# One attention block and one expert layer on one core: the transposes of the probabilities stand in front of the weighted sums instead of behind them

## The chip, the cores and the metric

The kernel runs on 1 core of one Trainium2 chip. The metric is the device time in microseconds (us) from start to end; lower is better. Engines are named as the profile names them: PE is TensorE (matmuls and transposes), PEld its weight loads, DVE is VectorE, ACT is ScalarE, POOL is GpSimd, SP issues DMAs.

## The reference

Two gated blocks follow each other on x of 32 batches x 128 tokens x 256.

```python
# cross attention, 16 heads of 64; scores and probabilities are 128 x 128 for each batch and head
q, k, v = layernorm(x) @ Wq, ctx @ Wk, ctx @ Wv
probs = softmax(q @ k.T / 8)
x = x + tanh(g_x) * ((probs @ v) @ Wo + bo)
# mixture of 8 experts, the best 2 for each token, with a capacity for each expert
logits = layernorm(x) @ gate_w.T
x = x + tanh(g_f) * sum over 2 experts of gate * (relu(row @ fc1 + b1) @ fc2 + b2)
```

## The kernel before

The attention takes the first 60% of the span, the experts the rest. The change is in the attention alone.

**Steps.** The 32 batches are 8 groups `g` of 4 (512 tokens). For a group the 16 heads go in 8 pairs, so there are 64 steps: step `u` is pair `j = u % 8` of group `u // 8`. In a step PE makes the queries of pair u, the keys of pair u+1 and a part of the values of step u+2, then the scores of pair u, and the weighted sums of pair u-2. `misc_of(u)` adds other work of a group's end to some steps: output projection (O0, O1), transposes for the second layer norm (XA, XB), routing (LT, LX, PR), and in the last step of a group (j = 7) the transposes FA and FB of the next group's normalised x.

**Order.** Each engine runs a program written out by hand, in order; engines tell each other by semaphores. Nothing is scheduled by a tool. PE's `step(u)` before: `transpose_probs(u-2)`, `query(u)`, keys, values, misc, `scores(u)`, `weigh_values(u-2)`. As the next step begins with `transpose_probs(u-1)`, PE meets scores (u), weighted sums (u-2), transposes (u-1), query products (u+1).

**Shapes in the PE array.** Query products and transposes use all 128 rows and columns of the array (128\*128 in the trace). The scores contract over 64, two heads side by side in the rows (64\*128). The weighted sums write 64 partitions, two heads side by side in the columns (128\*64). The names in the trace are `query_bank<-xT,w_split` (L515 to L517), `score<-k_sb,q_sb` (L598), `out_bank<-pT,v_sb` (L586, weighted sums), `probT<-ident,work` or `probs_odd` (L573, transposes).

**Around them.** DVE's step u: maxima of the scores of u-1 (L1025), `probs_out(u-2)`, which copies the two transposed banks `probT` to `pT` in SBUF (L1033), scaling of the first half of the probabilities u-1 by their sums (L1040), the low part of the attention output u-3 (`aT_l`, L904), scaling of the second half (L1040). In steps with j = 6 and 7 the routing stands between these; in steps with j = 7 the low parts `xT_l` of the next group's x follow. ACT's step u: exponentials of u-1 (L820), high part of the attention output u-3 (`aT_h`, L774), queries out (`q_sb`), keys and values out. `scores(u)` waits for `q_sb` and for the exponentials of u-1. `weigh_values` reads `pT`. `transpose_probs` waits for both scalings. There is one `pT` and one `out_bank`.

**After step 63** `finish()` transposes the probabilities of pair 62, does the weighted sums of 62 and 63 and projects the last group in pieces between them.

Of the kernel before, what the change touches and what calls it, by code (L numbers as in the profile page):

```python
# [132 lines left out]
def attention(nc, ctx, block, sem, x_v, out_v, disp, ctxT, g_x, g_f, wq, wk, wv, wo, bo, gateT, fc1T, fc2, shared):  # L133
# [86 lines left out]
    def misc_done(kind, g):  # L220

        return {
            "O0": (s_o_done, 2 * g - 1), "O1": (s_o_done, 2 * g), "XA": (s_xa_done, g), "XB": (s_xb_done, g),
            "LT": (s_lt_done, g), "LX": (s_lg_done, g), "PR": (s_pr_done, g), "GC": (s_gc_done, 1),
            "FA": (s_f_split, 2 * g + 3), "FB": (s_f_split, 2 * g + 4),
        }[kind]
# [274 lines left out]
    def _(pe):  # L501
# [64 lines left out]
        def transpose_probs(w):  # L566
            for hh in range(2):
                pe.wait_ge(s_p_ready, 2 * w + hh + 1)
                pe.wait_ge((s_pt_done0, s_pt_done1)[hh], w)
                if hh == 1 and w % NP == NP - 2 and w < STEPS - 2:  # L570
                    pe.wait_ge(*misc_done("FB", w // NP))
                for b in range(GB):
                    last = nc.tensor.transpose(probT[hh][:, b * P:(b + 1) * P], probs[w % 2][:, hh * GB + b, :], ident[:, :])  # L573
                last.then_inc(s_pt_ready, 1)
# [91 lines left out]
        def step(u):  # L666

            kinds, w, i = misc_of(u), u - 2, u + V_AHEAD
            if w >= 0:
                transpose_probs(w)  # L670
            query(u)
            if u == 0:
                keys_main(0)
                keys_rest(0)
                pe.wait_ge(s_v_done, 1)
                values_main(value_bank, i)
                keys_main(1)
            else:
                if u + 1 < STEPS:
                    keys_main(u + 1)  # L680
                if i < STEPS:
                    pe.wait_ge(s_v_done, i)
                    values_main(value_bank, i)
            if kinds:
                pe.wait_ge(s_q_done, u + 1)
                misc(kinds[0], query_bank, u // NP)
            if kinds[1:] == ["FB"]:
                pe.wait_ge(s_pt_done1, w + 1)
                misc("FB", probT[1], u // NP)
            elif kinds[1:]:  # L690
                pe.wait_ge(s_at_split, w)
                misc(kinds[1], out_bank, u // NP)
            if u + 1 < STEPS:
                keys_rest(u + 1)
            if i < STEPS:
                values_rest(value_bank, i)
            scores(u)
            if w >= 0:
                if kinds[1:] and kinds[1] != "FB":
                    pe.wait_ge(*misc_done(kinds[1], u // NP))  # L700
                else:
                    pe.wait_ge(s_at_split, w)
                weigh_values(w)
# [4 lines left out]
        def finish():  # L708

            def project_pairs(pairs, batches):  # L710

                for j in pairs:
                    pe.wait_ge(s_at_split, STEPS - NP + j + 1)
                    for b in batches:
                        o, t = last_bank(b)[:, 0:D], slice(b * P, (b + 1) * P)
                        mm(o, aT_h[:, j, t], wo_h[:, j, :], start=(j == 0), stop=False)
                        mm(o, aT_h[:, j, t], wo_l[:, j, :], start=False, stop=False)
                        last = mm(o, aT_l[:, j, t], wo_h[:, j, :], start=False, stop=(j == NP - 1))
                        if j == NP - 1 and b % 2 == 1:
                            last.then_inc(s_o_ready, 1)  # L720

            def transpose_x1(half):

                pe.wait_ge(s_o_done, 2 * NG - 1 + half)
                pe.wait_ge((s_pt_done0, s_pt_done1)[half], 8 * NG)
                for k in range(DK):
                    for b in range(2):
                        last = nc.tensor.transpose(probT[half][:, (2 * k + b) * P:(2 * k + b + 1) * P],
                                                   x1[:, 2 * half + b, k * P:(k + 1) * P], ident[:, :])
                last.then_inc(s_xt_ready, 1)  # L730

            def logits_half(half):

                pe.wait_ge(s_xa_done, NG + half)
                for b in (2 * half, 2 * half + 1):
                    for k in range(DK):
                        last = mm(out_bank[:, b * E:(b + 1) * E], xn2T[:, k, b * P:(b + 1) * P], gate_sb[:, k, :],
                                  start=(k == 0), stop=(k == DK - 1))
                last.then_inc(s_lg_ready, 1)

            early, late = (0, 1), (2, 3)
            transpose_probs(STEPS - 2)
            pe.wait_ge(s_v_done, STEPS)
            project_pairs((0, 1), early)
            pe.wait_ge(s_at_split, STEPS - 2)
            weigh_values(STEPS - 2)
            project_pairs((2, 3, 4, 5), early)
            transpose_probs(STEPS - 1)
            project_pairs((6,), early)
            pe.wait_ge(s_exp, 16 * NG)  # L750
            project_pairs((0,), late)
            weigh_values(STEPS - 1)
            project_pairs((1, 2), late)
            project_pairs((7,), early)
            project_pairs((3, 4), late)
            transpose_x1(0)
            project_pairs((5, 6), late)
            logits_half(0)
            project_pairs((7,), late)
            ranks(key_bank, halves[0], NG)  # L760
            transpose_x1(1)
            logits_half(1)
            pe.wait_ge(s_pr_done, NG)
            ranks(key_bank, halves[1], NG + 1)
            wait_warm(60)
# [6 lines left out]
    def _(act):  # L772
        def high(out_, in_, scale=1.0):
            return nc.scalar.activation(out_, in_, ACT.Copy, scale=scale)  # L774
# [60 lines left out]
        def step(u):  # L835

            g, kinds = u // NP, misc_of(u)
            if u > 0:
                exponentials(u - 1, 0)
            if u > 2:  # L840
                attention_high(u - 3)
            if u > 0:
                exponentials(u - 1, 1)
            act.wait_ge(s_q_ready, u + 1)
            high(q_sb[:, :], query_bank[:, :], SCALE).then_inc(s_q_done, 1)
            if "XA" in kinds:
                act.wait_ge(s_xt_ready, 2 * g - 1)
                high(xn2T[:, 0, :], query_bank[:, :]).then_inc(s_xa_done, 1)
            if "LT" in kinds:
                act.wait_ge(s_lt_ready, g)  # L850
                high(logitsT[:, :], query_bank[:, 0:P]).then_inc(s_lt_done, 1)
            if "PR" in kinds:
                act.wait_ge(s_gdiff, g)
                act.wait_ge(s_disp_done, g)
                nc.scalar.activation(packed[:, :, D + 1], route.gdiff[:, :], ACT.Exp).then_inc(s_gexp, 1)
            if g > 0 and u % NP == NP - 1:
                normalise_x1((2, 3), packed[:, 2:4], s_shift2, g).then_inc(s_xn2_ready, 1)
            if "FA" in kinds:
                for k in range(DK):
                    act.wait_ge(s_f_ready, 2 * g + 3 + k)  # L860
                    high(xT_h[:, k, :], (query_bank, probT[1])[k][:, :]).then_inc(s_f_hi, 1)
            if u == 0:
                keys_out(0)
            if u + 1 < STEPS:
                keys_out(u + 1)
            if u + V_AHEAD < STEPS:
                values_out(u + V_AHEAD)
            if "PR" in kinds:
                normalise_x1((0, 1), packed[:, 0:2], s_shift2, g)
            if u == 1:  # L870
                gates()
# [26 lines left out]
    def _(dve):  # L898
# [3 lines left out]
        def low(out_, full, high_):  # L902

            return V.tensor_tensor(out_, full, high_.bitcast(f32), ALU.subtract)  # L904
# [124 lines left out]
        def probs_out(w):  # L1029

            for hh, pt_done in enumerate((s_pt_done0, s_pt_done1)):
                dve.wait_ge(s_pt_ready, 2 * w + 1 + hh)
                V.tensor_copy(pT[:, hh, :], probT[hh][:, :]).then_inc(pt_done, 1)  # L1033

        def scale_probs(w, hh):
# [20 lines left out]
        def step(u):  # L1056
# [34 lines left out]
            if has_next and j == NP - 1:  # L1091
                for k in range(DK):
                    dve.wait_ge(s_f_hi, 2 * g + 3 + k)
                    low(xT_l[:, k, :], (query_bank, probT[1])[k][:, :], xT_h[:, k, :]).then_inc(s_f_split, 1)
            if has_prev and j == 2:
                residual_start(g)
                residual(g, query_bank, 0)
# [389 lines left out]
```

## Time and profile before

| what | value |
|---|---|
| median of 3 runs | 967.03 us (964.99 to 967.63) |
| profiled execution | 967.71 us, its span 966.0 us |
| PE busy | 942.8 us, 98% of the span |
| DVE busy | 654.8 us, 68% |
| ACT busy | 520.3 us, 54% |
| mean granted clock of TensorE | 0.989 of full speed |

A row of the timeline gives start, length, engine, line and operation, the tiles written and read, and how many instructions are merged; brackets at its end give the idle time before it and what ended it. A matmul's length reaches to its modelled end, and the next one starts before that, so of PE the starts are read. A share of busy time near 100% therefore says that nothing was waited for, not that no time is lost between matmuls.

### The profile page before, as it was taken

What the parts mean: (1) busy time and instruction counts of PE and PEld (TensorE: products, weight loads), DVE (VectorE), ACT (ScalarE), POOL (GpSimd) and SP (SyncE); (2) the same over time, 40 slices, a digit from 0 to 9 for tenths busy, and PEclk for the clock granted to TensorE, in tenths of its full rate; (3) what the DMA queues carried; (4) which work ended last, traced back from release to release, by engine and by line L of the source; (5) the groups of instructions that cost most, each with busy time, mean ns of one, the idle gap of its engine ahead of it and who ended that gap; (6) DMA issues with size and microseconds to landing.
All of it is one profiled execution on the core that took longest, in us unless ns stands there. A gap on an engine that the chain in (4) does not pass through costs nothing.

```text
span 966.0 us, 19023 instructions
## 1 busy us (share of the span) xinstructions
PE 942.8 (98%) x7221; PEld 826.1 (86%) x7221; DVE 654.8 (68%) x1533; ACT 520.3 (54%) x1611; POOL 282.8 (29%) x302
## 2 busy tenths in 40 slices
PE   8998999999999999999999889999999999999996
PEld 6787889889889888888898768999999999999995
DVE  3884795795885886867847756665757575757572
ACT  5774584783783774756847524343434343535351
POOL 5912024133142223243122340223232323222222
PEclk9999999999999999999999979999999999999998
DMA  9095320120021021012001114525252626252521
GB/s 267 12 295 134 110 66 30 39 67 35 34 73 61 2 77 57 25 45 64 13 34 45 43 59 164 137 44 137 45 141 41 147 42 147 46 146 56 128 45 22
DMA packets 63099, 76.65 MB, mean 79 GB/s; under 512 B 6030, under 2 KB 55093, under 8 KB 63008
## 3 DMA queue, kind: packets, MB, share of 16 engines
q1 hardware_dynamic: 50720, 59.18, 20.5%
q0 software_dynamic: 12288, 16.25, 9.2%
q8 instruction: 58, 0.95, 0.4%
q14 instruction: 33, 0.27, 0.1%
HBM read 46.52 MB, written 29.49 MB: 79 GB/s over the span
## 4 chain that ended last, share of the span: by engine, by line
PE 93%; DMA 2%; DVE 2%; ACT 1%; issue 0%; POOL 0%; DVEq 0%; POOLq 0%
PE probT L573 6%; PE down L1346 6%; PE down L1344 6%; PE down L1345 6%; PE out_bank L586 6%; PE up L1330 6%; PE up L1331 6%; PE up L1332 6%; PE score L598 6%; PE query_bank L515 3%; PE query_bank L517 3%; PE query_bank L516 3%; PE key_bank L540 3%; DMA rows<-x_dram 2%; PE probT L125 2%; PE rT L1314 1%
## 5 line engine op out<-in xcount | busy, mean ns | idle before, releaser
L1380 ACT ACTIVATE hid<-up,b 128x512 f32<-128x512 f32 x128 | 88.3, 690 | 203.7 <-PE up L1332 131.1
L1286 POOL DMA_INDIRECT out_dram<-eo,index x64 | 103.1, 1610 | 281.1 <-DVE eo L1448 249.7
L1025 DVE TENSOR_REDUCE negmax<-score 128x4 f32<-128x512 f32 x128 | 82.2, 684 | 42.3 <-PE score L598 42.2
L820 ACT ACTIVATE probs_odd<-score,negmax 128x128 f32<-128x128 f32 x256 | 91.1, 383 | 24.7 <-DVE negmax L1025 24.7
L774 ACT ACTIVATE k_sb<-key_bank 128x512 f32<-128x512 f32 x64 | 38.7, 604 | 120.8 <-PE key_bank L540 119.6
L419 POOL DMA_INDIRECT disp<-packed,slots x56 | 57.0, 1018 | 158.8 <-DMA disp<-packed,slots 108.1
L820 ACT ACTIVATE work<-score,negmax 128x128 f32<-128x128 f32 x256 | 91.2, 383 | 16.7 <-DVE negmax L1025 16.0
L1440 DVE TENSOR_TENSOR hid_l<-hid,hid_h 128x512 fp32r<-128x512 f32 x128 | 88.6, 692 | 4.4
L1033 DVE COPY pT<-probT 128x512 f32<-128x512 f32 x128 | 82.2, 683 | 13.4 <-PE probT L573 13.4
L1448 DVE SCALAR_TENSOR_TENSOR eo<-down,gate,shares_b 128x256 f32<-128x256 f32 x64 | 29.5, 481 | 85.4 <-PE down L1346 85.4
L1438 DVE CAST hid_h<-hid 128x512 fp32r<-128x512 f32 x128 | 55.5, 434 | 38.1 <-ACT hid L1380 36.5
L598 PEld LDWEIGHTS score<-k_sb,q_sb 64*128 64x128 f32 x1024 | 66.7, 187 | 7.1 <-ACT q_sb L774 4.7
L1344 PE MATMUL down<-w_h,hid_h 128*128 128x256 f32 x256 | 72.6, 284 | 0.0
L1344 PE MATMUL down<-w_split,hid_h 128*128 128x256 f32 x256 | 72.6, 284 | 0.0
L1346 PE MATMUL down<-w_h,hid_l 128*128 128x256 f32 x256 | 72.0, 281 | 0.0
L1345 PE MATMUL down<-w_l,hid_h 128*128 128x256 f32 x256 | 71.9, 281 | 0.0
L1345 PE MATMUL down<-w_split,hid_h 128*128 128x256 f32 x256 | 71.9, 281 | 0.0
L1346 PE MATMUL down<-w_split,hid_l 128*128 128x256 f32 x256 | 71.9, 281 | 0.0
L598 PE MATMUL score<-k_sb,q_sb 64*128 64x128 f32 x1024 | 68.5, 273 | 2.4 <-ACT q_sb L774 2.3
L586 PE MATMUL out_bank<-pT,v_sb 128*64 128x128 f32 x1008 | 69.0, 279 | 0.2 <-DVE aT_l L904 0.2
L586 PEld LDWEIGHTS out_bank<-pT,v_sb 128*64 128x64 f32 x1008 | 53.7, 136 | 7.9 <-DVE aT_l L904 0.4
L820 ACT ACTIVATION_READ_ACCUMULATOR work<-score,negmax 128x1 f32 x256 | 57.0, 223 | 0.0
(294 smaller groups left out, 2769.6 us busy)
## 6 DMA issues: line engine op xcount, KB each, us to landing
rows<-disp SPq DMA_DIRECT2D x18, 516.0 KB, 4.6
w_raw<-fc1T_dram SPq DMA_DIRECT2D x9, 1024.0 KB, 7.7
w_raw<-fc_dram SPq DMA_DIRECT2D x9, 1024.0 KB, 10.4
disp<-fixed SPq DMA_DIRECT2D x1, 8256.0 KB, 34.1
rows<-x_dram SPq DMA_DIRECT2D x16, 512.0 KB, 5.3
out_dram<-rows SPq DMA_DIRECT2D x8, 512.0 KB
c_raw<-ctxT_dram SPq DMA_DIRECT2D x8, 256.0 KB, 4.4
c_raw<-ctxT_dram SPq DMA_DIRECT2D x16, 128.0 KB, 5.0
```

Of the source, the lines that this page charges most:

```text
L573: last = nc.tensor.transpose(probT[hh][:, b * P:(b + 1) * P], probs[w % 2][:, hh * GB + b, :], ident[:, :])
L586: last = mm(bank[hh * DH:(hh + 1) * DH, b * P:(b + 1) * P], v_sb[:, j // 4, b, cols], pT[:, hh, b * P:(b + 1) * P], start=True, stop=True)
L598: last = mm(score[hh][:, t], q_sb[r, t], k_sb[u % 2][r, t], start=True, stop=True)
L820: last = nc.scalar.activation(probs[w % 2][:, c, :], score[hh][:, b * P:(b + 1) * P], ACT.Exp, bias=negmax[:, w % 2, c:c + 1], accum_out=s ...
L1025: V.tensor_reduce(negmax[:, w % 2, hh * GB:(hh + 1) * GB], score[hh][:, :].rearrange("p (i k) -> p i k", i=GB), axis=AX, op=ALU.max, negat ...
L1033: V.tensor_copy(pT[:, hh, :], probT[hh][:, :]).then_inc(pt_done, 1)
L1286: pool.indirect_dma_start(out=out_rows[:, :], out_offset=bass.IndirectOffsetOnAxis(ap=index[half][:, i:i + 1], axis=0), in_=eo[half][:, i, ...
L1344: mm(o, hid_h[:, k, t], w2_h[par][:, k, :], start=(k == 0), stop=False)
L1345: mm(o, hid_h[:, k, t], w2_l[par][:, k, :], start=False, stop=False)
L1346: last = mm(o, hid_l[:, k, t], w2_h[par][:, k, :], start=False, stop=(k == HK - 1))
L1380: nc.scalar.activation(hid[m % 2][:, :], up[m % 2][:, :], ACT.Relu, bias=b1[par][:, m:m + 1]).then_inc(s_hid, 1)
L1440: V.tensor_tensor(hid_l[:, m, :], hid[m % 2][:, :], hid_h[:, m, :].bitcast(f32), ALU.subtract).then_inc(s_hid_split, 1)
```

## The change

`transpose_probs` is called one step sooner, between `scores` and `weigh_values`. PE now meets scores (u), transposes (u-1), weighted sums (u-2), query products (u+1). Because the weighted sums of u-2 now come behind the transposes of u-1, DVE's copy of the new transposes waits until those sums have read `pT` (`s_av_ready`). FB no longer borrows `probT[1]` but `out_bank`: it waits for the attention output to be out of that bank, and the weighted sums of that step wait until FB has been read.

```diff
@@ transpose_probs
-                if hh == 1 and w % NP == NP - 2 and w < STEPS - 2:
-                    pe.wait_ge(*misc_done("FB", w // NP))
@@ step(u) of PE
-            if w >= 0:
-                transpose_probs(w)
             query(u)
...
-            if kinds[1:] == ["FB"]:
-                pe.wait_ge(s_pt_done1, w + 1)
-                misc("FB", probT[1], u // NP)
-            elif kinds[1:]:
+            if kinds[1:]:
                 pe.wait_ge(s_at_split, w)
                 misc(kinds[1], out_bank, u // NP)
...
             scores(u)
+            if w >= -1:
+                transpose_probs(w + 1)
             if w >= 0:
-                if kinds[1:] and kinds[1] != "FB":
+                if kinds[1:]:
                     pe.wait_ge(*misc_done(kinds[1], u // NP))
                 else:
                     pe.wait_ge(s_at_split, w)
@@ finish() of PE
-            transpose_probs(STEPS - 2)
@@ ACT, FA and FB
-                    high(xT_h[:, k, :], (query_bank, probT[1])[k][:, :]).then_inc(s_f_hi, 1)
+                    high(xT_h[:, k, :], (query_bank, out_bank)[k][:, :]).then_inc(s_f_hi, 1)
@@ probs_out(w) of DVE
                 dve.wait_ge(s_pt_ready, 2 * w + 1 + hh)
+                if w > 0:
+                    dve.wait_ge(s_av_ready, w)
                 V.tensor_copy(pT[:, hh, :], probT[hh][:, :]).then_inc(pt_done, 1)
@@ DVE, FA and FB
-                    low(xT_l[:, k, :], (query_bank, probT[1])[k][:, :], xT_h[:, k, :]).then_inc(s_f_split, 1)
+                    low(xT_l[:, k, :], (query_bank, out_bank)[k][:, :], xT_h[:, k, :]).then_inc(s_f_split, 1)
```

On PE, at the end of a plain step (the fifth, u = 4) and the start of the next, there stood before:

```order
107 L540 MATMUL key_bank<-c_d,wk_e 128x512
108 L559 MATMUL value_bank<-wv_e,c_t 128x512
109 L598 MATMUL score<-k_sb,q_sb 128x128 x8
110 L586 MATMUL out_bank<-pT,v_sb 64x128 x8
111 L573 MATMUL probT<-ident,probs_odd 128x128 x8
112 L515 MATMUL query_bank<-xT_h,w_split 128x512
```

Now there stands:

```order
107 L540 MATMUL key_bank<-c_d,wk_e 128x512
108 L559 MATMUL value_bank<-wv_e,c_t 128x512
109 L596 MATMUL score<-k_sb,q_sb 128x128 x8
110 L571 MATMUL probT<-ident,probs_odd 128x128 x8
111 L584 MATMUL out_bank<-pT,v_sb 64x128 x8
112 L515 MATMUL query_bank<-xT_h,w_split 128x512
```

The transposes and the weighted sums have changed places, and the query products now follow the weighted sums.

On PE, at the end of the second group (u = 15), the change gives this order, in which FB (the second row of L563) is in `out_bank` and the weighted sums (L584) wait for its readers:

```order
422 L563 MATMUL query_bank<-ident,rows 128x128 x4
423 L563 MATMUL out_bank<-ident,rows 128x128 x4
424 L540 MATMUL key_bank<-c_d,wk_e 128x512
425 L559 MATMUL value_bank<-wv_e,c_t 128x512
426 L596 MATMUL score<-k_sb,q_sb 128x128 x8
427 L571 MATMUL probT<-ident,work 128x128 x8
428 L584 MATMUL out_bank<-pT,v_sb 64x128 x8
```

Before, the second row of L563 wrote `probT`, and the last two rows stood the other way round.

On DVE the order is the same; only the copy of `probT` has one more wait:

```order
36 L1019 TENSOR_REDUCE negmax<-score 128x4 [waits a_s_ready] x2
37 L1029 COPY pT<-probT 128x512 [waits a_av_ready,a_pt_ready] x2
38 L1034 RECIPROCAL rsum<-sums 128x4 [waits a_exp]
39 L1036 TENSOR_TENSOR probs_odd<-probs_odd,rsum 128x512 [waits a_dve_self]
```

## Rows read from the trace of the kernel before

**Rows 1.** The page, part 1: busy time and share of each engine.

```profile
PE 942.8 (98%) x7221; PEld 826.1 (86%) x7221; DVE 654.8 (68%) x1533; ACT 520.3 (54%) x1611; POOL 282.8 (29%) x302
```

**Rows 2.** Timeline of PE, end of step 2 and start of step 3.

```profile
32.87 1.06 PE L598 MATMUL score<-k_sb,q_sb 64*128 64x128 f32 x16
33.85 1.09 PE L586 MATMUL out_bank<-pT,v_sb 128*64 128x128 f32 x16
34.88 1.09 PE L573 MATMUL probT<-ident,probs_odd 128*128 128x128 f32 x8
35.73 0.47 PE L515 MATMUL query_bank<-xT_h,w_split 128*128 128x512 f32 x1
36.04 0.39 PE L516 MATMUL query_bank<-xT_l,w_split 128*128 128x512 f32 x1
```

**Rows 3.** Timeline of PE, end of steps 0 and 1 (no weighted sums).

```profile
21.94 1.05 PE L598 MATMUL score<-k_sb,q_sb 64*128 64x128 f32 x16
22.92 0.50 PE L515 MATMUL query_bank<-xT_h,w_split 128*128 128x512 f32 x1
23.26 0.40 PE L516 MATMUL query_bank<-xT_l,w_split 128*128 128x512 f32 x1
...
27.20 1.16 PE L598 MATMUL score<-k_sb,q_sb 64*128 64x128 f32 x16 [0.38 <-ACT q_sb L774]
28.29 1.10 PE L573 MATMUL probT<-ident,work 128*128 128x128 f32 x8
```

**Rows 4.** Timeline of PE in finish(): projection, weighted sums, projection.

```profile
550.74 0.28 PE L718 MATMUL score<-w_split,aT_l 128*128 128x256 f32 x1
550.95 1.09 PE L586 MATMUL key_bank<-pT,v_sb 128*64 128x128 f32 x16
551.97 0.39 PE L716 MATMUL score<-w_split,aT_h 128*128 128x256 f32 x1
```

**Rows 5.** Timeline of DVE, steps 3 and 4.

```profile
35.57 1.29 DVE L1033 COPY pT<-probT 128x512 f32<-128x512 f32 x2 [0.33 <-PE probT L573]
...
39.56 0.69 DVE L1040 TENSOR_TENSOR work<-work,rsum 128x512 f32<-128x512 f32 x1
```

**Rows 6.** Timeline of ACT, step 3.

```profile
36.06 0.61 ACT L774 ACTIVATE aT_h<-out_bank 128x512 fp32r<-128x512 f32 x1
```

**Rows 7.** Timeline of all engines, end of step 9.

```profile
82.13 0.66 PE L573 MATMUL probT<-ident,work 128*128 128x128 f32 x4
83.67 0.75 DVE L908 BATCH_NORM_STATS2 stats<-rows 128x6 f32<-128x256 f32 x2 [4.72 <-DMA rows<-x_dram]
...
85.28 0.98 PE L573 MATMUL probT<-ident,work 128*128 128x128 f32 x4 [2.50 <-DVE work L1040]
```

**Rows 8.** Window behind that wait (last: granted clock, DMA share, GB/s).

```profile
85.40:88.90 3.50, 3.50 (x11) 2.92 (x12) 3.47 (x7) 3.04 (x16) 1.80 (x2) 0.51 0.08 27
```

**Rows 9.** Timeline of PE and DVE, steps 15 and 16.

```profile
139.22 1.09 PE L586 MATMUL out_bank<-pT,v_sb 128*64 128x128 f32 x16
...
139.75 0.68 DVE L904 TENSOR_TENSOR xT_l<-probT,xT_h 128x512 fp32r<-128x512 f32 x1
...
144.47 0.50 PE L540 MATMUL key_bank<-c_d,wk_e 64*128 64x512 f32 x1
...
145.00 1.16 PE L598 MATMUL score<-k_sb,q_sb 64*128 64x128 f32 x16
```

**Rows 10.** Timeline of PE and DVE, step 52.

```profile
453.10 1.05 PE L598 MATMUL score<-k_sb,q_sb 64*128 64x128 f32 x16
...
454.16 0.69 DVE L1040 TENSOR_TENSOR probs_odd<-probs_odd,rsum 128x512 f32<-128x512 f32 x1
```

**Rows 11.** Timeline of PE and DVE, step 63 and finish().

```profile
539.98 1.16 PE L598 MATMUL score<-k_sb,q_sb 64*128 64x128 f32 x16 [1.96 <-ACT q_sb L774]
...
543.99 0.68 DVE L904 TENSOR_TENSOR aT_l<-out_bank,aT_h 128x512 fp32r<-128x512 f32 x1
...
544.73 1.09 PE L586 MATMUL out_bank<-pT,v_sb 128*64 128x128 f32 x16 [0.15 <-DVE aT_l L904]
```

## Prediction

> **What bounds the kernel now.** I read the page first. PE is busy 98% of the span and DVE 68% [rows 1]. Almost nothing is waited for on PE, so time can only be won or lost in what PE's own instructions cost, and in the few places where it does wait. The change adds and removes no matmul, no copy and no DMA. It is a question of order.
>
> So the second view is the timeline of PE around the place of the change, read by the starts. In a plain step the scores start at 32.87, the weighted sums at 33.85, the transposes at 34.88, the query products at 35.73, and the second query product at 36.04 [rows 2]: 0.98, 1.03, 0.85 and 0.31 us, 3.17 together. These distances are not all work. The 16 scores last 1.06 with a modelled length of 0.27 for one (my reading of a single matmul; the sum needs only starts), so their last one starts about 0.79 behind the first, at 33.66. The first weighted sum starts 0.19 later, though within the group one starts every 0.05. The last weighted sum starts about 0.82 behind the first, at 34.67, and the first transpose again 0.21 later. But the last of the 8 transposes starts at about 35.70, and the first query product 0.03 later. The array's shape changes at the first two places (64\*128 to 128\*64, 128\*64 to 128\*128) and not at the third. That is what I build on: a change of shape costs about 0.15 to 0.2 us of PE, hidden by nothing, in a stage that PE bounds.
>
> This is also what the Trainium skill says in "TensorEngine Tiling (Array Packing)", Key Properties: changing the tiling mode, and not only the tile, drains the engine. It speaks against this change and gives no figure; the trace agrees, with some 0.20 us between last and first start at a change of shape and 0.03 us where none is.
>
> **The change part by part: the swap on PE.** Before, a step has the shapes 128\*128 (queries, keys, values), 64\*128 (scores), 128\*64 (sums), 128\*128 (transposes, then queries): three changes. Now it is 128\*128, 64\*128 (scores), 128\*128 (transposes), 128\*64 (sums), 128\*128: four. The trace has no step in the new order, but it has nearly each seam.
>
> - Scores to a 128\*128 shape: 0.98 in step 0, from 21.94 to 22.92, where query products follow at once [rows 3]. The transposes of step 1 also follow scores, 1.09 behind a group that had a wait of its own inside [rows 3]. I take 0.98, as to the weighted sums.
> - Transposes to weighted sums: 0.82 from first to last transpose, and then the seam. A 128\*128 projection before weighted sums shows 0.21, from 550.74 to 550.95 [rows 4]. Together 1.03.
> - Weighted sums to a 128\*128 shape: 1.03 to transposes [rows 2], 1.02 to the projection, from 550.95 to 551.97 [rows 4]. I take 1.03.
> - First to second query product behind a change of shape: 0.34, from 22.92 to 23.26 [rows 3], instead of 0.31.
>
> The sum is 0.98 + 1.03 + 1.03 + 0.34 = 3.38 us against 3.17: **0.21 us more** for each swap. Bounds: nothing, if no seam costs by shape, and 0.30, if the two unseen seams cost half as much again as those seen.
>
> **Where it counts.** There are 62 swaps, one behind the scores of each step from 2 to 63. Not all of them lie on the path.
>
> - Steps 2 to 8 (7 swaps, 1.5 us): at the end of step 9 PE waits 2.50 us in the middle of the transposes, for a scaling that DVE does only behind statistics of x that a DMA brings at 83.67 [rows 7]. DVE had been idle for 4.72 us for that load. The end of the wait is set by the load, so these 1.5 us vanish in it: 0. If the load came later because its issue waits for FB (5 swaps ahead of it), it would be 1.0; I take 0, as it lands 16 us after PE's work for it, behind other transfers.
> - Step 9: the weighted sums stood ahead of this wait and now stand behind it. That costs their 1.03, the seam before them (0.21 instead of 0.03), and 0.03 behind: **+1.2 us**.
> - Steps 10 to 60: 51 swaps by 0.21, **+10.7 us**.
> - Steps 61 and 62: the scores of step 63 wait 1.96 us for ACT's `q_sb` [rows 11], a chain that comes from DVE and ACT. Both swaps are covered: 0. Without that cover 0.4.
>
> **The new waits.** (a) DVE's copy of the transposes now waits for the weighted sums, which end last. Before, it started at 35.57, with the first four transposes done [rows 5]. Now the sums start at 32.87 + 0.98 + 1.03 = 34.88 and end 1.09 later, so the copy starts at 36.0 to 36.05: 0.45 later. Behind it on DVE are the scalings of the next probabilities. The second one starts at 39.56 and lasts 0.69 [rows 5], so it ends at 40.25, or 40.7 if nothing absorbs the delay. The new transposes come 0.98 behind scores that start one step after 32.87, at 39.45 to 39.7; their second half needs this scaling 0.44 after that, near 41.0. Cover 0.3 or more: cost 0. (b) ACT's high part of the attention output starts at 36.06 [rows 6], when its exponentials are done; the sums now end at about 36.0. Cost 0. (c) In step 52 DVE is late: the second scaling ends at 454.85 [rows 10]. The new transposes' second half could start at 453.10 + 0.98 + 0.44 + 0.21 = 454.7. With the 0.45 of (a) it waits until 455.3: **+0.6**. Before, the weighted sums covered this. (d) FB in `out_bank`: weighted sums of the last step of a group wait for `xT_l`, which ends at 140.43 [rows 9], or 140.75 with DVE some 0.3 later. They could start at 139.22 + 1.03 + 0.21 = 140.45. That is 0.3 to 0.35 of new wait in the five groups with routing on both sides. But the scores of the next step then waited already: they started 0.53 behind the last part of the keys (144.47 to 145.00) [rows 9], where 0.33 is usual, and 0.1 more inside. A PE that comes later doesn't wait there. Net 0 to -0.1 each: **-0.5** for all. (e) In `finish()` the weighted sums of 62 wait for the low part of 61, made at 543.99 behind the copy of the transposes, and start at 544.73 [rows 11]. That copy is 0.45 later as in (a), and so are they: **+0.5**.
>
> **Sum:** 10.7 + 1.2 + 0.6 - 0.5 + 0.5 = 12.5 us on the profiled execution, which took 967.7 us (span 966.0). That execution is 0.7 us above the median of 967.0, so I forecast 967.0 + 12.5, about **979.5 us**.
>
> One thing can take back a part: behind the 2.50 us wait the granted clock was 0.51 for 3.5 us, near the lower of its two levels (1.2 of 2.4 GHz) [rows 8], which cost about 1.4 us. The wait changes too: the sums no longer stand ahead of it, and PE comes to it 1.5 us later, so it is 2.50 + 1.03 - 1.5 = 2.0 us. With less idle time the clock may not fall: -1.4. A wait of 1.96 us [rows 11] is as long, and I leave it open.
>
> **The rivals.**
>
> - *DVE becomes the bound.* The 0.45 us of (a) goes round: copy, scaling, transposes, and the second half of the transposes waits in each step. For it: DVE's chain from score to scaling takes most of a step. Against it: the cover of 0.3 worked out above, which grows by 0.21 with each slower step of PE. Price: 0.25 more in 51 steps, 12.8 us, 992 us. It decides from the point where DVE's second scaling comes over 0.3 later than I think.
> - *The seam isn't due to the shape*, but belongs to any group behind several waits, and the order changes nothing on PE. Then only the stalls remain: 1.2 - 0.2 + 0.6 - 0.5 + 0.5 = 1.6 us, 968.6 us. Against it: transposes and query products also have waits in front, and there it is 0.03.
> - *Faster: a drain is paid only between the two split shapes.* If transposes to sums and sums to query products came at the group's own pace (0.05 instead of 0.2 at both seams), a step would be 0.98 + 0.87 + 0.88 + 0.31 = 3.04, 0.13 less than before. 51 times that is -6.6, with 1.6 of stalls: 962 us. It decides from the point where both seams together are under 0.22. Against it are sums to projection, 1.02 [rows 4], and scores to query products, 0.98 [rows 3], which show the full seam. The one seam never seen is transposes to sums.
>
> **How the numbers follow.** My forecast (four changes of shape instead of three) has 0.80, DVE as the bound 0.08, no change on PE 0.07, faster 0.05. A change of 0.3% (2.9 us) is about what a measurement of this kernel can tell from none. Slower by more: 0.80 + 0.08 = 0.88. Within: 0.07. Faster: 0.05. The range of the likeliest case: from 0.15 for a swap (7.7 instead of 10.7) and a clock that doesn't fall, 967.0 + 12.5 - 3.0 - 1.4 = 975, to 0.26 for a swap, the load 1.0 later and 1 us of waits more, 984. I give 973.5 to 985, a little wider for the waits that I took as covered.
>
> **What would show it.** In the trace after: scores to transposes 0.98, transposes to sums 1.03, sums to query products 1.03 by the starts, and a plain step 0.21 us longer. The copy of `probT` starts 0.45 later behind the scores. PE's waits stay few: the one at the end of step 9 near 2.0 us, one in step 52, short ones at L584 in the last step of a group. If transposes follow scores with a wait for L1036 in most steps, the first rival holds. If a plain step is as long as before, the second. What would make the prediction wrong is above all a seam from transposes to sums that costs much more or much less than the 0.21 of a projection.

## The result

The changed kernel takes 977.29 us in the median of 6 runs (975.27 to 978.68). The kernel before, run beside it, took 966.01 us (6 runs, 964.46 to 967.63). The ratio is 1.0116, with a 95% interval of 1.0100 to 1.0131: 9.7 to 12.7 us slower. The forecast was 979.5 us from a base of 967.0, which is 12.5 us slower, or a ratio of 1.013. The profiled execution spans 977.0 us, 11.0 more than before.

PE's time in the page grew by the same 11 us, and PE is still busy 98% [rows 1]:

```profile
PE 953.9 (98%) x7221; PEld 828.5 (85%) x7221; DVE 653.6 (67%) x1533; ACT 521.3 (53%) x1611; POOL 280.4 (29%) x302
```

The timeline of PE at the end of step 2 of the changed kernel answers to [rows 2]:

```profile
32.65 1.06 PE L596 MATMUL score<-k_sb,q_sb 64*128 64x128 f32 x16
33.64 1.09 PE L571 MATMUL probT<-ident,probs_odd 128*128 128x128 f32 x8
34.66 1.09 PE L584 MATMUL out_bank<-pT,v_sb 128*64 128x128 f32 x16
35.68 0.50 PE L515 MATMUL query_bank<-xT_h,w_split 128*128 128x512 f32 x1
36.02 0.40 PE L516 MATMUL query_bank<-xT_l,w_split 128*128 128x512 f32 x1
```

Read by the starts: 0.99, 1.02, 1.02 and 0.34 us, 3.37 together, where the forecast had 3.38 and before it was 3.17. No bracket stands at any of these rows: nothing is waited for, and the time is lost all the same. From the scores of one plain step to those of the next it is 0.18 to 0.20 us more than before, throughout the attention (step 27 to 28: 248.65 to 255.96, 7.31; before 244.25 to 251.38, 7.13).

These are all of PE's waits over 0.3 us in the changed kernel (in total, times, longest):

```profile
PE key_bank L125 <- POOLq L340: 3.7, 1, 3.7
PE probT L571 <- DVE work L1036: 2.8, 2, 2.6
PE key_bank L618 <- DVE mask_half L958: 2.5, 2, 1.7
PE score L596 <- ACT q_sb L768: 1.8, 2, 1.5
PE probT L723 <- DVE rows L1127: 0.8, 1, 0.8
PE out_bank L732 <- ACT work L768: 0.7, 1, 0.7
PE probT L571 <- DVE probs_odd L1036: 0.5, 1, 0.5
PE out_bank L584 <- DVE aT_l L898: 0.5, 1, 0.5
```

The wait of 2.6 is the one at the end of step 9 (2.50 before, [rows 7]; the forecast had 2.0), the one of 0.5 for `probs_odd` is that of step 52, the one of 0.5 for `aT_l` that of `finish()`. The timeline around the wait of step 9, PE and DVE of the changed kernel:

```profile
82.41 0.66 PE L571 MATMUL probT<-ident,work 128*128 128x128 f32 x4
84.06 0.75 DVE L902 BATCH_NORM_STATS2 stats<-rows 128x6 f32<-128x256 f32 x2 [3.49 <-DMA rows<-x_dram]
...
85.67 0.66 PE L571 MATMUL probT<-ident,work 128*128 128x128 f32 x4 [2.61 <-DVE work L1036]
...
86.25 1.97 PE L584 MATMUL out_bank<-pT,v_sb 128*64 128x128 f32 x16
```

The weighted sums now come behind the wait. They also last 1.97 instead of 1.09, since the granted clock has fallen: a window from 86 to 88 us reads 0.56.

DVE's copy starts later behind the scores by 0.53 us, where 0.45 was expected. It started 2.70 us behind them (32.87 to 35.57, [rows 5]) and now 3.23 (32.65 to 35.88):

```profile
35.88 1.29 DVE L1029 COPY pT<-probT 128x512 f32<-128x512 f32 x2 [0.85 <-PE out_bank L584]
```

### The profile page after: what moved, and what is told of

Its sections match the earlier page's. It is cut to its first block, busy times and chain, and to the rows that moved or that the text cites. A ratio compares the mean times of both kernels' runs of the same rounds, so it can differ in the third digit from the quotient of the medians.

```text
span 977.0 us, 19149 instructions
## 1 busy us (share of the span) xinstructions
PE 953.9 (98%) x7221; PEld 828.5 (85%) x7221; DVE 653.6 (67%) x1533; ACT 521.3 (53%) x1611; POOL 280.4 (29%) x302
## 4 chain that ended last, share of the span: by engine, by line
PE 94%; DVE 3%; DMA 2%; issue 1%; ACT 0%; POOL 0%; DVEq 0%; POOLq 0%
PE out_bank L584 6%; PE probT L571 6%; PE down L1342 6%; PE down L1340 6%; PE down L1341 6%; PE up L1326 6%; PE up L1327 6%; PE up L1328 6%; PE score L596 5%; PE query_bank L515 4%; PE query_bank L516 3%; PE query_bank L517 3%; PE key_bank L540 3%; DMA rows<-x_dram 2%; PE probT L125 2%; PE rT L1310 1%
## 5 line engine op out<-in xcount | busy, mean ns | idle before, releaser
L1019 DVE TENSOR_REDUCE negmax<-score 128x4 f32<-128x512 f32 x128 | 82.2, 683 | 34.1 <-PE score L596 34.1
L584 PE MATMUL out_bank<-pT,v_sb 128*64 128x128 f32 x1008 | 69.8, 281 | 0.6 <-DVE aT_l L898 0.5
L584 PEld LDWEIGHTS out_bank<-pT,v_sb 128*64 128x64 f32 x1008 | 54.4, 138 | 11.4 <-issue 9.5
L515 PE MATMUL query_bank<-xT_h,w_split 128*128 128x512 f32 x128 | 57.4, 449 | 0.0
```

What stands on the lines that cost most here:

```text
L515: mm(query_bank[:, :], wq_h[:, k, c], xT_h[:, k, :], start=(k == 0), stop=False)
L584: last = mm(bank[hh * DH:(hh + 1) * DH, b * P:(b + 1) * P], v_sb[:, j // 4, b, cols], pT[:, hh, b * P:(b + 1) * P], start=True, stop=True)
L1019: V.tensor_reduce(negmax[:, w % 2, hh * GB:(hh + 1) * GB], score[hh][:, :].rearrange("p (i k) -> p i k", i=GB), axis=AX, op=ALU.max, negat ...
```

## The experiments

Each was run beside the kernel before. For the mixed orders, `swapped(u)` says in which steps the transposes stand ahead of the weighted sums.

**Where the swaps count.** Three kernels with the new order in some steps, DVE's added wait, and FB as before:

```diff
+        def swapped(u):
+            return 2 <= u <= 8          # s2_8; in s9: u == 9; in s10_60: 10 <= u <= 60 and u % NP != NP - 1
-            if w >= 0:
+            if w >= 0 and not swapped(u - 1):
                 transpose_probs(w)
             query(u)
...
             scores(u)
+            if swapped(u):
+                transpose_probs(w + 1)
             if w >= 0:
```

*Steps 2 to 8.* 

> The new order in steps 2 to 8 alone (7 swaps), FB as before. All theories agree on +0.19 us a swap up to the scores of step 9, +1.3 us there. Theory A (the wait at the end of step 9 is ended by a load that lands at its own time): the wait is shorter by 1.3 us, the scores of step 10 come 0.0 to 0.2 us later than before, the whole is the same within 0.3%. Theory B (the load lands later with its issue, which waits for FB behind 5 swaps): the scores of step 10 come 0.9 us later. Theory C (nothing absorbs them): 1.3 us later.

Measured: 966.81 us (10 runs) against 966.52 (25 runs), ratio 0.9998 (0.9983 to 1.0013), so -1.6 to +1.3 us. The swaps cost nothing that can be told. C's 1.3 us lies at the very end of the interval; B's 0.9 is not excluded by the times. The profile doesn't show the absorption: in that execution the load was there at 82.65 us, sooner than before, PE came later, and it didn't wait at all, so the scores of step 10 started at 100.61 in place of 102.32. The wait that was to absorb the swaps is itself of changing length. Against B, that the load lands later when it is issued later, speak the traces of SP: its issue starts at 66.74 us in the kernel before, 66.07 with step 9 alone, 68.92 here and 69.06 in the second profile of the changed kernel (below), and DVE's statistics that wait for it start at 83.67, 82.65, 82.65 and 82.43. An issue 3 us later is not followed by a later landing.

*Step 9.* 

> The new order in step 9 alone, FB as before. Theory A: the weighted sums no longer stand ahead of the wait of 2.5 us but behind it; the wait reads 3.5 us and the scores of step 10 come 1.2 us later than before (1.03 for the sums, 0.2 for the seam). If the clock's lower stretch behind the wait grows or moves, up to 0.6 us more. A theory in which only the number of seams counts: 0.2 us later.

Measured: 968.38 us (10 runs), ratio 1.0015 (0.9999 to 1.0031), 1.4 us by the ratio, with an interval of -0.1 to +3.0 (the medians are 1.9 apart). The timeline of PE shows the mechanism: the first four transposes, the wait, and the sums behind it.

```profile
80.44 0.66 PE L573 MATMUL probT<-ident,work 128*128 128x128 f32 x4
84.26 0.66 PE L573 MATMUL probT<-ident,work 128*128 128x128 f32 x4 [3.17 <-DVE work L1047]
84.85 1.23 PE L586 MATMUL out_bank<-pT,v_sb 128*64 128x128 f32 x16
```

The wait is 3.17 us where 3.5 was expected. The load landed sooner than before, as the timeline of DVE shows:

```profile
82.65 0.75 DVE L913 BATCH_NORM_STATS2 stats<-rows 128x6 f32<-128x256 f32 x2 [4.37 <-DMA rows<-x_dram]
```

So the size has to be read from the landing. In all three profiles, before, changed and this one, the transposes go on 1.61 us behind the start of these statistics. The scores of step 10 follow the statistics by 18.65 us before (83.67 to 102.32), by 19.83 here (82.65 to 102.48) and by 19.83 in the changed kernel (84.06 to 103.89): 1.18 us more, twice, against the 1.2 of the forecast and the 0.2 of a theory in which only the seams count. The granted clock fell in all three. The scatter of the old order is not small beside that: the kernel with four more waits (below) also has the old order here and a late load, and shows 18.22 (84.15 to 102.37).

*Steps 10 to 60 without the last of each group.* 

> The new order in steps 10 to 60 without those with j = 7: 45 swaps, FB as before. Theory A (one more change of the array's shape in each, 0.19 us): 45 x 0.19 = 8.6 us, 0.5 us for a wait in step 52, and about 0.3 us less at each of five group ends where waits of before are absorbed: +7.5 to +8.5 us. Theory D (the cost comes from the copies of probT that start 0.45 us later, as a chain through DVE): the cost would sit in waits for DVE that add up to most of 8 us; A expects under 2 us of them.

Measured: 975.04 us (4 runs) against 966.52, ratio 1.0080 (1.0053 to 1.0107), so 5 to 10 us with 7.7 by the ratio. From the scores of step 10 to those of step 63 the profile shows 445.97 us against 437.66, +8.3. The waits of PE from 110 to 530 us are a single row, while the 8 us are there: theory D, which puts them into waits for DVE, is out.

```profile
PE probT L573 <- DVE probs_odd L1047: 0.5, 1, 0.5
```

**All but the swap.** The changed kernel with `transpose_probs(w + 1)` put back behind `weigh_values(w)`.

```diff
             scores(u)
-            if w >= -1:
-                transpose_probs(w + 1)
             if w >= 0:
...
                 weigh_values(w)
+            if w >= -1:
+                transpose_probs(w + 1)
```

> All of the change but the swap: FB in out_bank, DVE's added wait, transposes behind the weighted sums. Theory A: shapes and their number as before, so plain steps last as long as before; but the weighted sums of the last step of a group wait for xT_l with no transposes ahead of them, 1.2 us in five groups and 0.3 to 0.4 in two, of which 0.3 us each is given back in the next step: +4 to +5 us. A theory in which the move of FB is free: 0. It tells what part of the 11 us isn't the swap's.

Measured: 971.77 us (10 runs), ratio 1.0049 (1.0036 to 1.0062), 3.5 to 6.0 us. Plain steps last as before to 0.01 us. The step with the group's end is 1.07 us longer. Its row in the timeline of PE:

```profile
138.85 1.09 PE L584 MATMUL out_bank<-pT,v_sb 128*64 128x128 f32 x16 [1.19 <-DVE xT_l L898]
```

The row of PE's waits over the whole, in seven places (five of about 1.2 us, two short ones):

```profile
PE out_bank L584 <- DVE xT_l L898: 6.5, 7, 1.2
```

**The swap alone.** The other half: all 62 swaps, FB in `probT[1]` as before, and one `transpose_probs(STEPS - 2)` less in `finish()`.

```diff
+            return 2 <= u < STEPS
...
-            transpose_probs(STEPS - 2)
             pe.wait_ge(s_v_done, STEPS)
```

> All 62 swaps, but FB stays in probT[1], so that the second half of the transposes waits for xT_l in the last step of a group. Against before. Theory A: the 11 us of the whole change, and 0.9 to 1.1 us more in five group ends, because the transposes (0.44 us of them) and not the whole group now stand ahead of that wait: +14 to +16 us. If FB's move costs in the changed kernel what it costs alone (4 to 5 us), then this one is at +6.

Measured: 979.31 us (4 runs) against 965.18 (21 runs), ratio 1.0144 (1.0129 to 1.0160), +14 us. The waits between 110 and 530 us are now for `xT_l`, 0.6 us in five steps:

```profile
PE probT L573 <- DVE xT_l L908: 2.8, 5, 0.6
PE probT L573 <- DVE probs_odd L1046: 0.3, 1, 0.3
```

In each of these five the step is 0.64 to 0.68 us longer than in the changed kernel, less than the 0.9 to 1.1 expected. So FB's move costs 4.7 us by itself (1.0049 of 966.5) and is worth 3 us inside the change (1.0144 against 1.0116; from the scores of step 10 to those of step 63 the profiles read 450.08 and 446.71, 3.4 apart). The two edits belong together: with the transposes in front, the wait for `xT_l` is covered, and in the changed kernel only 0.1 us of it is left (the weighted sums of step 15 start 1.12 us behind the transposes instead of 1.02).

**What the seam costs, and why.** Two kernels set the shape of the array against the number of waits. In the first the changed kernel takes transposes and sums in turns:

```diff
+                transpose_probs(w + 1, (0,))
...
-                weigh_values(w)
+                weigh_values(w, (0, 1))
+                transpose_probs(w + 1, (1,))
+                weigh_values(w, (2, 3))
```

> From the changed kernel: transposes and weighted sums in turns (4 transposes, half of the sums, 4 transposes, the other half), so two more changes of the array's shape in each of 62 steps, no wait added that isn't long satisfied, and the same work. Theory A (0.19 us for each further change of shape): a plain step is 0.38 us longer than in the changed kernel, over some 53 steps that aren't covered +20 us on it, +31 us on before. Theory E (the gap belongs to a group behind several waits of its own): the added half of the sums repeats waits that are long satisfied, so at most 0.19 us a step, +10 us on the changed kernel or none.

Measured: 992.01 us (4 runs), ratio 1.0262 (1.0238 to 1.0287) to the kernel before, 25.5 us above it and 15 above the changed kernel beside it (976.87, one run). That is between the 10 and the 20 of the two theories, so both sizes were missed. The timeline of PE says why:

```profile
48.22 0.66 PE L571 MATMUL probT<-ident,probs_odd 128*128 128x128 f32 x4
48.81 0.66 PE L584 MATMUL out_bank<-pT,v_sb 128*64 128x128 f32 x8
49.40 0.65 PE L571 MATMUL probT<-ident,probs_odd 128*128 128x128 f32 x4
49.98 0.66 PE L584 MATMUL out_bank<-pT,v_sb 128*64 128x128 f32 x8
50.57 0.50 PE L515 MATMUL query_bank<-xT_h,w_split 128*128 128x512 f32 x1
```

From the first transposes to the query product it is 2.35 us, where the changed kernel has 2.04 (33.64 to 35.68): 0.31 for two further changes of shape, 0.15 each. That is the gap of 0.20 less the pace of 0.05 that would stand there anyway. My 0.19 was that of the swap, which makes the second query product 0.03 later as well.

There is a row in which these seams can be counted. PEld, the weight loads, stands idle for 0.17 us ahead of the first load at each seam behind transposes or weighted sums, and its list of waits puts that down to "issue" (in total, times, longest). Before:

```profile
PEld probT L573 <- issue: 10.6, 62, 0.2
```

The changed kernel:

```profile
PEld query_bank L515 <- issue: 10.8, 62, 0.3
PEld out_bank L584 <- issue: 9.5, 57, 0.2
```

The kernel with turns:

```profile
PEld out_bank L584 <- issue: 19.9, 118, 0.2
...
PEld query_bank L515 <- issue: 10.7, 62, 0.2
PEld probT L571 <- issue: 10.4, 61, 0.2
```

62 places before, 119 in the changed kernel, 241 with turns. It is a count and not the price, and the seam behind the scores isn't in it.

But the kernel with turns repeats the waits of the sums too, so the second one takes them alone, where no shape changes:

```diff
             if w >= 0:
                 transpose_probs(w)
+            if w >= 1:
+                pe.wait_ge(s_at_split, w - 1)
+                pe.wait_ge(s_v_done, u - 1)
+                pe.wait_ge(s_pt_done0, w)
+                pe.wait_ge(s_pt_done1, w)
             query(u)
```

> The kernel before, with four satisfied waits of the weighted sums repeated between the transposes and the query products, where no change of shape is. Theory A: last transpose to first query product stays 0.03 us, the whole is the same within 0.3%. Theory E (several waits ahead of a group make the gap): about 0.15 us more in each of 61 steps, +9 us.

Measured: 967.15 us (10 runs) against 966.51 (19 runs), ratio 1.0004 (0.9988 to 1.0020). The timeline of PE in step 2:

```profile
33.90 1.06 PE L598 MATMUL score<-k_sb,q_sb 64*128 64x128 f32 x16
34.88 1.09 PE L586 MATMUL out_bank<-pT,v_sb 128*64 128x128 f32 x16
35.91 1.09 PE L573 MATMUL probT<-ident,probs_odd 128*128 128x128 f32 x8
36.76 0.47 PE L515 MATMUL query_bank<-xT_h,w_split 128*128 128x512 f32 x1
37.07 0.39 PE L516 MATMUL query_bank<-xT_l,w_split 128*128 128x512 f32 x1
```

0.98, 1.03, 0.85, 0.31: as before. The added waits are in the program as it ran (its trace has 122 instructions more, two for each of 61 steps). Four more satisfied waits cost nothing that can be measured, and theory E is out.

**Is the wait at the end of step 9 on the path?** The kernel before with one scaling moved on DVE:

```diff
+            if u == NP + 1:
+                scale_probs(u - 1, 1)
             if has_next and j == (1 if has_prev else 2):
                 dve.wait_ge(s_x_in, 16 * g + 32)
...
-            if u > 0:
+            if u > 0 and u != NP + 1:
                 scale_probs(u - 1, 1)
```

> The kernel before, in which DVE's step 9 does the second scaling ahead of the statistics of x that wait for the load. Nothing else is moved. The transposes no longer wait 2.5 us for it and the clock needn't fall behind them (about 1.4 us): -3 to -4 us if the load's lateness isn't handed on to the scores of step 10, which have 12 us of projection ahead of them; 0 if it is. It tests whether that wait is on the path at all, as the absorption of the first swaps says.

Measured: 965.23 us (10 runs) against 966.51, ratio 0.9985 (0.9972 to 0.9998), 0.2 to 2.7 us faster and less than the 3 to 4 expected. The wait of step 9 is gone, but a part comes back as a wait of the projection for `q_sb` (PE's waits):

```profile
PE query_bank L611 <- ACT q_sb L774: 1.6, 1, 1.6
```

In this profile the rest was lost at another place. The timeline of PE, step 63:

```profile
538.16 1.37 PE L598 MATMUL score<-k_sb,q_sb 64*128 64x128 f32 x16 [1.97 <-ACT q_sb L774]
539.46 1.97 PE L586 MATMUL out_bank<-pT,v_sb 128*64 128x128 f32 x16
```

Behind the wait ahead of the scores of step 63 the weighted sums last 1.97 us where the kernel before had 1.09. The window of 5 us from those scores (granted clock, DMA share and GB/s last) reads, in this kernel:

```profile
538.16:543.16 5.00, 5.00 (x44) 4.44 (x45) 3.15 (x10) 2.60 (x10) 2.55 (x3) 0.66 0.14 49
```

and in the kernel before:

```profile
539.98:544.98 5.00, 4.84 (x56) 4.36 (x58) 4.57 (x13) 3.69 (x16) 2.56 (x3) 1.00 0.14 49
```

The order of the instructions is the same there. The changed kernel was profiled once more in this place: 

> The changed kernel once more, beside the others on this chip: about +11 us, for a second reading of the wait at the end of step 9 (2.6 us in its first profile).

Measured: 976.87 us (one run), 10.4 above the kernel before beside it. The load came early, PE waited 0.2 us in step 9 instead of 2.6, and its clock didn't fall. From the scores of step 10 to those of step 63 it is 446.67 us, in the first profile 446.71. From there to the end it is 427.6 us, where the first profile had 426.4. ACT's last high part of the attention output starts 15.10 us behind the scores of step 63 instead of 13.00, although the weighted sums that it reads end at about 13.4, and PE waits for what DVE makes of it:

```profile
PE query_bank L711 <- DVE aT_l L898: 1.5, 1, 1.5
```

The granted clock is 1.00 there in both. Why ACT starts later in some executions stays open; the same wait, 1.0 to 1.6 us, stands in the profiles of steps 2 to 8, steps 10 to 60, all but the swap, the swap alone and scaling first.

**A clock that falls in some executions.** The window behind the scores of step 63 read 0.66 in five of the seven profiles with the old order there (steps 2 to 8, steps 10 to 60, all but the swap, waits, scaling first) and 1.00 in two (before, step 9). With the new order it read 1.00 in all four, behind a wait of 1.2 to 1.5 us instead of 2.0. From those scores to the next weighted sums but one (the first in `finish()`) it is 4.75 us in the two profiles at 1.00 and 6.2 to 6.4 in the five at 0.66, so the fall costs 1.4 to 1.6 us. From those scores to the end it is 426.0 us in the first two and 427.4 to 428.1 in the five; but that stretch also holds the late start of ACT told above, which made it 427.6 and 428.1 in two profiles whose clock did not fall (the changed kernel's second, the swap alone). To try whether work in the wait prevents the fall:

```diff
+            if u == STEPS - 1:
+                pe.wait_ge(s_v_done, STEPS)
+                keep_warm(nc, value_bank, wk_h[:, 0:P], wk_h[:, 0:TOK], 7)
             scores(u)
```

> The kernel before with 7 matmuls without use, 1.6 us, into the free value bank, in the wait of 2.0 us ahead of the scores of step 63. Theory F (behind this wait the granted clock falls in 5 of 7 profiles in the old order, which costs 1.7 us there): about 1 us faster in the median, 0.1%, and the granted clock of the next 5 us is 1.00. If the fall comes all the same: 0, or 0.1 us slower.

Measured: 964.23 us (11 runs) against 965.18 (21 runs), ratio 0.9991 (0.9982 to 1.0000). 

> The same, and the second scaling of step 9 ahead of the statistics that wait for x. Theory F and the reading that the wait of step 9 is on the path: 2 to 3 us faster than before, 0.2 to 0.3%, the fastest of all. If gains ahead of step 10 are lost again later: as warm alone.

Measured: 963.50 us (11 runs), ratio 0.9980 (0.9971 to 0.9989), 1.1 to 2.8 us faster than before and the lowest median of all. The windows behind the scores of step 63 in the two:

```profile
536.89:541.89 5.00, 4.87 (x56) 4.38 (x58) 4.57 (x13) 3.69 (x16) 2.56 (x3) 1.00 0.13 45
```

```profile
536.72:541.72 5.00, 4.87 (x56) 4.38 (x58) 4.58 (x13) 3.69 (x16) 2.56 (x3) 1.00 0.13 45
```

Both read 1.00, and both times agree with a fall prevented. But two of seven profiles read 1.00 without any such work, so two more don't prove it, and the gain of the first kernel has an interval that reaches to nothing.

## Why the prediction was right

The likeliest case came, and its cause is shown: one more change of the array's shape in each step, in a stage that PE bounds. Two further changes of shape cost 0.31 us together, waits added without a shape cost nothing that can be measured, and a swap in the plain steps costs its 0.19 us with no wait for DVE. The forecast of 12.5 us was 1.2 above the 11.3 between the medians. The 9 us of steps 10 to 60 stand in both profiles of the changed kernel; what comes ahead of them and behind them changes from one execution to the next, and that it adds up to little is in part luck.

By the terms of the sum, against the first profile of the changed kernel:

- *A swap, 0.21.* Measured 0.19. The three seams were as taken from the neighbours; the never seen one, transposes to sums, is 1.02 against 1.03. One thing was told wrongly: the keys and values do not stay at 128\*128, their last parts are 64\*128 like the scores [rows 9], so that change of shape lies ahead of them. It is there in both kernels and changes nothing in the sum.
- *Steps 10 to 60, 10.7 + 0.6 - 0.5 = 10.8.* Measured 433.56 us from the scores of step 10 to those of step 61 (103.89 to 537.45) against 424.52: +9.0 (433.51 in the second profile). In it are 51 swaps by 0.19, 9.7; step 52 with 0.5 instead of 0.6 (its step is 0.68 longer, less the swap); and, as what is left over, the group ends with about -1.2 instead of -0.5. There I had mis-sized two things: the weighted sums wait 0.1 us for `xT_l` and not 0.3 to 0.35, and small waits for `q_sb` ahead of FA vanish too (0.4 us of the weight loads in each of six places before, none after).
- *Step 9, +1.2.* In this profile the scores of step 10 come 1.6 us later than before, 0.4 of it because the load landed later (84.06 against 83.67); counted from the landing it is 1.18, as in the kernel with the new order in step 9 alone. So mechanism and size are right where the load is late. In the second profile of the changed kernel it landed at 82.43, PE waited 0.2 us, and this term wasn't paid. The wait forecast as 2.0 us was 2.6 and 0.2.
- *Steps 2 to 8, nothing.* Timed as 0 (-1.6 to +1.3), which fits. From the scores of step 2 to those of step 9 it is 1.5 us more, as priced; they can vanish only in an execution in which PE then waits for the load.
- *Steps 61 and 62, nothing.* Measured 0.01 us each.
- *finish(), +0.5.* The wait for `aT_l` is 0.47 us, and 0.15 before [rows 11]; from the scores of step 63 to the end it is 0.4 us more (426.4 and 426.0). In the second profile it is 1.6 more (427.6), for the late start of ACT.
- *The clock, left open.* In step 9 it fell in the first profile and not in the second: there it scatters from one execution to the next. Behind the scores of step 63 it fell in none of the four profiles with the new order and in five of seven with the old; up to about 1 us in the median (five of seven times 1.5) could come of that in favour of the change, which isn't shown and wasn't in the sum.

Of the rivals, DVE as the bound didn't come: in the second profile as in the first, PE's waits between 110 and 530 us are 0.5 to 0.6 us in one place. Its 0.45 us of delay was 0.53, and is covered but for some 0.2 us in single steps (step 3, and those with j = 6) and the 0.5 of step 52. That the seam isn't due to the shape is refuted by the kernel with four more waits, and that a drain is paid only between the two split shapes is refuted by the starts in the changed kernel (1.02 and 1.02).

## What to carry to other kernels

Where PE is busy without a gap, look at the starts of its matmuls and not at its busy share: at each change of the array's shape (64\*128, 128\*64, 128\*128) time is lost that no wait of PE shows, and it is paid as often as the loop runs. The weight loads' list of waits counts a part of such places, here those behind transposes and weighted sums. Order the groups so that equal shapes stand side by side, before thinking of which result is wanted sooner. And when a group is moved past another one, look for the waits that the other covered: each of the two edits here was dearer alone than with its partner.

## What the runs showed of the hardware that I had not expected

A change of shape between groups of 128-column matmuls costs 0.15 us of PE over the pace of the group (0.31 us for two). I had expected some such price, but not that the starts would be the same to one or two hundredths behind scores, transposes and weighted sums (0.98 or 0.99, 1.02, 1.02) and from one plain step to the next. It isn't the same everywhere: ahead of the last part of the keys, behind matmuls of 512 columns that start every 0.23 us, the change to 64\*128 takes 0.31 from start to start, 0.08 over the pace. The timeline of PE, step 2 of the changed kernel:

```profile
32.00 0.39 PE L553 MATMUL value_bank<-wv_d,c_d 128*128 128x512 f32 x1
32.31 0.49 PE L540 MATMUL key_bank<-c_d,wk_e 64*128 64x512 f32 x1
```

Behind a wait of PE of 2.0 us at one and the same place, with the same instructions around it, the granted clock fell to a mean of 0.66 over 5 us in five executions and stayed at 1.00 in two. The fall costs 1.4 to 1.6 us there. The executions also differ ahead of anything that was changed: the scores of step 2 start between 32.2 and 34.1 us in the thirteen traces. Two profiles can thus differ by some us for no reason that lies in the change, and one should compare stretches between such places (446.67 and 446.71 us) rather than spans.
